# Where the value products of a group of heads are computed in a fused transformer kernel on one Trainium2 core

## The reference

```
x = x + attention(layernorm(x), Wq, bq, Wk, bk, Wv, bv, Wo, bo, gq, gk)
q = h @ Wq + bq;  k = h @ Wk + bk;  v = h @ Wv + bv     # 1024x512 @ 512x4096
q = rms_norm(q, gq);  k = rms_norm(k, gk)               # over all 4096 columns
out = softmax(q @ k.T / sqrt(128)) @ v                  # per head of 128 columns
return out @ Wo + bo
```

## Time and profile before

| | us |
|---|---|
| median of 3 runs (lowest, highest) | 2278.64 (2277.76, 2283.53) |
| the profiled execution | 2280.5 |
| its span, first to last instruction | 2278.7 |
| PE busy in the span | 2213.6 |
| DVE busy | 1710.7 |
| ACT busy | 1233.3 |
| POOL busy | 972.3 |
| mean granted TensorE clock | 0.99 |

### The profile page before, as it was taken

One profiled execution on the slowest core, in us unless ns is written; L12 is line 12 of the kernel. 1 busy time (PEld: TensorE's weight loads), 2 busy tenths in 40 slices (PEclk: granted clock), 3 DMA queues, 4 the chain that ended last, 5 costly groups with the idle time before them and its releaser, 6 DMA issues. The chain is left out here.

```text
span 2278.7 us, 34738 instructions
## 1 busy us (share of the span) xinstructions
PE 2213.6 (97%) x10852; PEld 1836.1 (81%) x10852; DVE 1710.7 (75%) x2796; ACT 1233.3 (54%) x2094; POOL 972.3 (43%) x863
## 2 busy tenths in 40 slices
PE   7989999999999999999999999999999999899998
PEld 5778888888788888888888888888877788687886
DVE  5677667766588888888888888888875676784665
ACT  3365555554466666666666666666653343351442
POOL 5577666665322222222122122222215476672565
PEclk9999999999999999999999999999999999899999
DMA  4066666555412212212212112112101020140210
GB/s 135 10 205 200 201 203 201 190 188 173 159 64 84 74 51 83 74 51 83 72 52 83 63 61 83 56 68 83 53 12 61 33 84 31 36 139 28 75 61 37
DMA packets 108488, 210.47 MB, mean 92 GB/s; under 512 B 9985, under 2 KB 42753, under 8 KB 107137
## 3 DMA queue, kind: packets, MB, share of 16 engines
q1 hardware_dynamic: 108416, 209.58, 27.5%
HBM read 140.33 MB, written 69.21 MB: 92 GB/s over the span
## 5 line engine op out<-in xcount | busy, mean ns | idle before, releaser
L1559 ACT ACTIVATE at_pT_hi<-ps 128x512 fp32r<-128x512 f32 x512 | 278.2, 595 | 355.4 <-PE ps L1668 355.4
L1602 DVE TENSOR_REDUCE softmax<-ps 128x1 f32<-128x1024 f32 x254 | 310.1, 1221 | 84.3 <-PE ps L421 83.4
L1613 DVE TENSOR_TENSOR at_pT_lo<-ps,at_pT_hi 128x512 fp32r<-128x512 f32 x512 | 327.2, 680 | 2.0 <-ACT at_pT_hi L1559 2.0
L421 PE MATMUL ps<-ln_xT_hi,first_parts 128*128 128x512 f32 x656 | 222.7, 401 | 7.1 <-DVE ln_xT_lo L292 4.0
L1498 POOL TENSOR_TENSOR at_o_lo<-at_o_raw,at_o_hi 128x512 fp32r<-128x512 f32 x32 | 41.3, 1292 | 431.6 <-ACT at_o_hi L1581 431.6
L421 PE MATMUL ps<-ln_xT_hi,queries 128*128 128x512 f32 x816 | 221.5, 391 | 0.0
L1628 DVE SCALAR_TENSOR_TENSOR x<-ps,softmax,x 128x512 f32<-128x512 f32 x256 | 192.1, 750 | 8.0 <-PE ps L421 3.1
L421 PE MATMUL ps<-ln_xT_hi,ln_xT_lo 128*128 128x512 f32 x768 | 196.0, 390 | 0.0
L1693 PE MATMUL ps<-at_pT_hi,ln_xT_lo 128*128 128x512 f32 x512 | 180.6, 393 | 0.6 <-DVE at_y_lo L1598 0.6
L421 PEld LDWEIGHTS ps<-ln_xT_hi,queries 128*128 128x128 f32 x816 | 153.5, 188 | 32.8
L421 PEld LDWEIGHTS ps<-ln_xT_hi,ln_xT_lo 128*128 128x128 f32 x768 | 144.2, 188 | 30.8
(11 more groups left out here) (314 smaller groups left out, 5779.3 us busy)
## 6 DMA issues: line engine op xcount, KB each, us to landing
scratch_v<-v_res SPq DMA_DIRECT2D x64, 256.0 KB, 2.3
scratch_q_hi<-qkv_q_hi SPq DMA_DIRECT2D x64, 256.0 KB, 2.3
scratch_q_lo<-qkv_q_lo SPq DMA_DIRECT2D x64, 256.0 KB, 2.6
scratch_k<-qkv_res SPq DMA_DIRECT2D x64, 256.0 KB, 3.0
keys<-scratch_k SPq DMA_DIRECT2D x32, 512.0 KB, 3.8
at_v_raw<-scratch_v SPq DMA_DIRECT2D x32, 512.0 KB, 3.3
wv_raw<-in_Wv SPq DMA_DIRECT2D x8, 1024.0 KB, 6.2
first_raw<-in_Wqk SPq DMA_DIRECT2D x16, 512.0 KB, 3.7
```

The costliest lines, as they stand in the source:

```text
L421: last = nc.tensor.matmul(out, s, m, start=(start and n == 0), stop=(stop and n == len(terms) - 1), skip_group_check=more)
L1559: nc.scalar.activation(pT2[jp][0][:, 4 * b:4 * b + 4, w * P:(w + 1) * P], T_BANKS[:, b * HALF:(b + 1) * HALF].rearrange("p (k n) -> p k n" ...
L1602: nc.vector.reduce_max(maxes[:, l % 4:l % 4 + 1], scores(l)[:], AX.X).then_inc(s_max, count(i, l))
L1613: nc.vector.tensor_tensor(pT2[jp][1][out], T_BANKS[:, b * HALF:(b + 1) * HALF].rearrange("p (k n) -> p k n", k=4), pT2[jp][0][out], ALU.su ...
```

## The change

The tail of every group but the first now has all eight value units, that of group 0 its units 5 to 7; no value unit is left in a first pair, nor its eviction or store. The four blocks of value weights are rounded behind pair 0 (blocks 0 and 1), pair 1 (block 2) and pair 2 (block 3).

```diff
-        QUADS, UNITS, EARLY, BODY = 4, 8, 5, 6
+        QUADS, UNITS, EARLY, BODY = 4, 8, 5, 8
-        VALUE_PARTS = {0: (0, 1), 2: (2, 3)}
+        VALUE_PARTS = {0: (0, 1), 1: (2,), 2: (3,)}
@@ -1197,8 +1197,6 @@
                     elif is_first(g):
                         evict_values(0, FIRST)
-                    else:
-                        evict_values(g - 1, BODY)
                     keep_u2(g, j)
...
                     elif is_first(g):
                         evict_values(0, FIRST + 1)
-                    else:
-                        evict_values(g - 1, BODY + 1)
@@ -1329,9 +1325,7 @@
                         fourth(g, j - 1)
-                    elif not is_first(g):
-                        values_unit(g - 1, BODY)
-                    else:
+                    elif is_first(g):
                         pe.wait_ge(t_lo_done, 2)
...
                     times(d_bank(j), j, S1, T1).then_inc(p5_done, 1)
-                    if j == 0 and not is_first(g):
-                        values_unit(g - 1, BODY + 1)
```

## The result

The kernel after takes **2295.26 us** (median of 5 runs, 2292.37 to 2299.43), the kernel before beside it 2278.76 (5 runs, 2277.76 to 2283.53): ratio 1.0069, 95% interval 1.0056 to 1.0082, slower by 16.5 us. That is slower by more than 0.3%, as forecast; the forecast of 2288.7 fell 6.6 us short. The measured time lies inside the stated range, but that range, 2275.8 to 2299, also held every rival; the narrower one of the forecast itself, 2284 to 2298, holds it too. The 43 runs of before that were made later, beside the experiments, have medians of 2282.17 and 2281.77, against which 2295.26 is 13 us more; so some 3 of the 16.5 us are not firm.

The account below looks back on a forecast made before the run. PE's matmuls and the holes between them were taken to bound the kernel. Per group 1.7 + 0.1 - 0.35 = 1.45 us, over seven groups 10.1 us on the median 2278.64, gave 2288.7 us; range 2275.8 to 2299.

Parts of the forecast that it names:

- What bounds the kernel: Groups of heads: PE is busy nearly throughout; 264 matmuls take 59.8 of 60.2 us, the rest is one hole.
- (a): Two value units move from first pair to tail: PE's work unchanged, 0 us; the pair's cover shrinks from 12.2 to 6.8 us.
- (b): Short first pair: DVE's earliest-due results stay covered, by 0.3 us for one product and 0.8 for the next pair's first matmul.
- (c): First pair's later work: DVE and POOL block each other, making DVE 2.0 to 2.1 us late in pair 1.
- (d): End of pair 1: new ACT rounding adds 0.57 us; lateness 2.7 against slack 1.0, so PE waits 1.7 us.
- The other path: Key store to a product of pair 2: slack 0.5 us, a 1.6 us wait under the same hole, counted once.
- (e): Second value rounding leaves pair 2, so its fourth product no longer waits: minus 0.35 us per group.
- 1.45 us per group, seven groups: Groups 1 to 7: 1.7 + 0.1 for the refill - 0.35, together 10.1 us.
- A: First pair: weight load lands late, DVE gets through ahead of POOL, not slower; 2276.2 us, chance 0.18.
- B: Groups: gain and loss cancel, DVE under 1.0 us late and slack absorbs it; 2277 to 2284 us, chance 0.25.
- C: Behind the new hole PE's clock drops, losing 1.5 us each of seven times; 2299 us, chance 0.07.

Follow-up runs that it names:

- POOL-short kernel: Kernel after, with nearly all of POOL's weight sums and adds of squares cut to 2 columns from group 1 on; 2278.28 us, ratio 0.9986.
- units-only kernel: Kernel after, with the value weights rounded behind pairs 0 and 2 as before, so only the value units moved; 2297.33 us, ratio 1.0074.
- the three places alone: Kernel before, with only the value roundings spread behind pairs 0, 1 and 2, value units left in place; 2277.09 us, ratio 0.998.

## Why the prediction came out as it did

**What bounds the kernel** held: PE's matmuls and the holes between them, 59.84 us for a group without one.

**(a), (b)** held. S3 and p1(1) of the short pair were not late in groups 1 to 7 of any kernel.

**(c)** held nearly to the tenth: the C22 eviction was forecast 11.8 us after p1(0) and came at 11.66, u2 of pair 1 at 7.6 after p1(1) and came at 7.3. The two rows that already held the turns priced them right; the POOL-short kernel shows 3.2 us of turns in that stretch. What the reading left out stood in its own numbers. C22 evicted at 11.8 us ends at 12.4, and third(0), which adds to that bank, is due at 12.2. The forecast followed C22 on DVE to u2, and did not ask PE. This is 0.27 us a group, 1.9 us over seven.

**(d)** held in place and cause: the hole at fourth(1), released by ACT L966, forecast 1.7 + 0.1 us, measured 1.53 + 0.11. u3 was 2.8 us late (forecast 2.7), but fourth(1) had been moved by the small hole before it, so the sum of the two was right. That 2.7 was so near is in part luck: DVE was 1.7 us late at u2, not 2.0 to 2.1, and 0.6 more came from one turn more in pair 1, which the forecast had only in its upper bound. The other path, key store to S3(2), stayed just under it in the regular groups: DVE waited 0.63 us for the store (258.21) instead of 2.38. In the units-only kernel it came out, as the forecast had it.

One reading in (d) was right in number and wrong in weight: the new rounding was counted as 0.57 of the lateness. With it moved back the group became longer by 0.54 us, because S3(2) and fourth(2) then had holes. It adds to the hole at fourth(1), and saves more than that behind it.

**(e)** held: 0.34 us measured alone in group 2, 0.35 forecast. Only in group 7 of the kernel after does fourth(2) wait again.

**The sum.** The term that was mis-sized is "1.45 us per group, seven groups". It was 1.7 to 1.9 in groups 2 to 6: 0.27 at third(0), 1.64 at fourth(1), some 0.16 in small spacings, less 0.34. In group 1 it was 2.46, with the slow DMA issue, and 2.33 in group 7, which has 0.46 us more in a hole at fourth(2) (574.30). Together 13.8 against 10.1. The last 3.0 us between the two spans lie outside these groups: 0.76 ahead of the stage, 0.9 in group 0, 1.35 behind the sums. All three are within the scatter of the same programs shown under the result, so the forecast was right to have nothing there. In group 0 it is the clock: behind its hole of 3.7 us 12 matmuls ran in 5 us at a granted clock of 0.50, where before had 15 at 0.66.

**The rivals.** A was false: the weight load of pair 2 landed 4.0 us after its issue and POOL came first. B fell with it; one unit moved instead of two would have given it, ratio 0.9998. C was false: behind holes of 1.5 to 1.6 us the granted clock stayed 1.00 in each of groups 1 to 7. The Trainium skill (Perfetto Trace Analysis, Optimizing Scalar/DVE Operations) says that breaking up instructions on ScalarE or VectorE that cause bubbles elsewhere may let work be completed sooner. No instruction was split here, only the places of four were spread, so the prediction took the advice in a wider sense; in that sense it held, since the three places alone won 0.2%. It says nothing against the other half, which lost 0.7%.

## What to carry to other kernels

Work inside a pipeline that looks as if it could stand anywhere may be the cover of two other engines: before it is moved, add up what those engines must finish under it, and take durations from rows where both are busy, since here a blocked instruction was shown as busy. When DVE and POOL block each other, putting one off can move the turns to the next pair with the same deadline, as it did here; only fewer turns or more cover helped. And follow a late eviction to every product that adds to its bank, the nearest first.

## What the runs showed of the hardware

The same two 128x512 DVE subtractions took 1.28 us with POOL waiting or short, 2.37 beside its sums of weights (0.9 to 1.2 us each as shown, 0.73 at 233.74 in before, where DVE was idle) and 3.46 beside its adds of squares (1.6 to 1.7 us each as shown, 1.29 without DVE in the way): 0.54 and 1.09 us for each turn. The loss follows the length of the other engine's instruction. The forecast had priced turns, but not that they add up to the tenth within a pair.

Issuing the key store of pair 1 took SP 1.46 to 2.16 us in group 1 of five kernels, against 0.39 to 0.41 in their groups 2 to 6. Slow issues are not rare: in before seven other key stores between 164 and 513 us took 0.96 to 1.46 us, and no matmul started late behind them. It mattered where it fell on the key store of pair 1.

Behind 3.10 us of idle PE the granted clock fell in before, to 0.66 over 5 us. In the kernel after, 3.05 us of it at the same place did not lower it. The ten traces go five to five there: it fell behind 3.05, 3.05, 3.07, 3.10 and 3.15 us, and stayed up behind 3.05 (four times) and 3.07. PE's timeline, kernel after:

```profile
118.25 0.47 PE L421 MATMUL ps<-qkv_right_hi,qkv_left_hi 128*128 128x512 f32 x1 [3.05 <-ACT rk L960]
...
122.51 0.47 PE L421 MATMUL ps<-qkv_right_hi,qkv_left_hi 128*128 128x512 f32 x1 [1.25 <-DVE keys L1101]
```

Twelve matmuls ran at 0.24 us, and then S3 waited for DVE's u2. From the end of the hole to that S3 matmul are 4.26 us here and 4.41 in before (117.54 to 121.95), where the same twelve ran slowly and nothing waited. So the low clock cost 0.15 us there, not the 1.5 that rival C was priced with, since what stood behind it was late anyway. At the hole of 3.7 us in group 0 the clock fell in both kernels; windows view of the 5 us behind it, kernel after:

```profile
145.56:150.56 5.00, 5.00 (x12) 3.93 (x13) 4.88 (x6) 3.60 (x8) 4.36 (x5) 0.50 0.49 183
```
